# A fused pair-update and feed-forward kernel: the mix stage reads a transposed, normalized x stored by the projection stage instead of making its own

## What is computed

```
zn = LN(LN_c(x)); ppn, lpn, ipn = LN of the three other grids
ab1, ab2, ab3 = sigmoid(zn@Wg_k + bg_k) * (zn@W_k + b_k) * mask          (64 channels each)
pp, lp, ip    = the same form on the three others, without the mask
block = einsum('ikc,kjc->ijc', pp, ab1) + einsum('ikc,jkc->ijc', ab2, lp) + ab3*ip
g     = sigmoid(zn@Wend + bend)
x2    = x + g * (LN(block)@Wsum + bsum) * mask
t     = LN(x2); logits = mean(t)@Wr + br -> two of eight experts
out   = x2 + LN(t + expert mixture(t)) * gamma + beta
```

## Time and profile before

| | |
|---|---|
| time, median of 3 runs | 1593.93 us (1591.71 to 1597.03) |
| the profiled execution's own time | 1593.88 us |
| its span | 1592.1 us |
| PE busy | 1420.5 us (89%) |
| DVE busy | 1247.0 us (78%) |
| ACT busy | 1060.3 us (67%) |
| POOL busy | 1061.2 us (67%) |
| DMA | 232.66 MB, 347992 packets |

### The profile page before, as it was taken

One profiled execution on the slowest core, in us unless ns is written; L12 is line 12 of the kernel. 1 busy time (PEld: TensorE's weight loads), 2 busy tenths in 40 slices (PEclk: granted clock), 3 DMA queues, 4 the chain that ended last, 5 costly groups with the idle time before them and its releaser, 6 DMA issues. The chain is left out here.

```text
span 1592.1 us, 34869 instructions
## 1 busy us (share of the span) xinstructions
PE 1420.5 (89%) x10157; PEld 1186.6 (75%) x10157; DVE 1247.0 (78%) x4401; ACT 1060.3 (67%) x2439; POOL 1061.2 (67%) x1691
## 2 busy tenths in 40 slices
PE   6999999999999997787779999869999999999992
PEld 3877777777777776666657777649998888898882
DVE  7898888888888865555579999857788888888874
ACT  3877877877877883222279999734666667667662
POOL 4888888888888894333269999823555555555553
PEclk9999999999999998998989999969999999999996
DMA  9878789887899877676636665321222222222212
GB/s 197 201 180 200 183 205 225 203 192 179 188 206 222 207 201 215 191 244 174 175 86 176 167 179 166 107 74 37 67 80 67 79 79 69 76 79 66 80 41 79
DMA packets 347992, 232.66 MB, mean 146 GB/s; under 512 B 59558, under 2 KB 331902, under 8 KB 347838
## 3 DMA queue, kind: packets, MB, share of 16 engines
q1 hardware_dynamic: 346556, 230.40, 56.0%
q10 hardware_dynamic: 1010, 0.20, 0.1%
q0 software_dynamic: 272, 0.21, 0.1%
HBM read 155.28 MB, written 75.50 MB: 145 GB/s over the span
## 5 line engine op out<-in xcount | busy, mean ns | idle before, releaser
L616 PE MATMUL psZ_a<-w_all,xT_a 128*128 128x128 f32 (+1 forms) x2304 | 453.6, 336 | 33.9 <-ACT xT_a L526 23.3
L616 PEld LDWEIGHTS psZ_a<-w_all,xT_a 128*128 128x128 f32 x2304 | 316.1, 196 | 84.9 <-ACT xT_a L526 28.3
L1461 ACT ACTIVATE hT<-psH_d,b 128x512 f32<-128x512 f32 x288 | 197.7, 688 | 172.2 <-PE psH_d L1501 172.1
L1486 PE MATMUL psY_d<-w,hT 128*128 128x128 f32 x2304 | 268.9, 275 | 0.0
L1486 PEld LDWEIGHTS psY_d<-w,hT 128*128 128x128 f32 x2304 | 262.9, 192 | 0.1
L542 ACT ACTIVATE sig_a<-psZ_a 128x256 f32<-128x256 f32 (+1 forms) x360 | 153.4, 426 | 95.9 <-PE psZ_a L616 54.4
L1519 POOL TENSOR_TENSOR u_d<-u_d,gamma 128x512 f32<-128x512 f32 x72 | 95.6, 1328 | 159.9 <-ACT u_d L1447 142.3
L603 PE MATMUL psT_a<-ident,shared 128*128 128x128 f32 x1152 | 189.0, 277 | 4.2 <-issue 2.8
L603 PEld LDWEIGHTS psT_a<-ident,shared 128*128 128x128 f32 x1152 | 143.8, 144 | 55.5 <-issue 27.9
L554 POOL TENSOR_SCALAR shared<-shared,coefs_ix 128x128 f32<-128x128 f32 x348 | 154.0, 454 | 45.1 <-DVE coefs_ix L360 42.8
L526 ACT COPY xT_a<-psT_a 128x512 f32<-128x512 f32 (+1 forms) x360 | 175.9, 489 | 4.2 <-PE psT_a L603 2.5
(11 more groups left out here) (221 smaller groups left out, 3071.2 us busy)
## 6 DMA issues: line engine op xcount, KB each, us to landing
shared<-in_x_dram SPq DMA_DIRECT2D x48, 512.0 KB, 4.9
scratch_x<-x_c SPq DMA_DIRECT2D x36, 512.0 KB, 3.1
shared<-scratch_x SPq DMA_DIRECT2D x36, 512.0 KB, 3.6
shared<-in_x_dram SPq DMA_DIRECT2D x48, 256.0 KB, 4.3
shared<-L_conv_protein_pair_dram SPq DMA_DIRECT2D x24, 512.0 KB, 7.6
shared<-in_L_conv_l_pair_dram SPq DMA_DIRECT2D x24, 512.0 KB, 6.4
shared<-n_L_conv_inter_pair_dram SPq DMA_DIRECT2D x24, 512.0 KB, 6.4
scratch_ab<-low_ab SPq DMA_DIRECT2D x12, 1024.0 KB, 5.7
```

What stands on the lines that cost most here:

```text
L616: ins = nc.tensor.matmul(out, xT[:, G % 2, j * P:j * P + P], rhs[i], start=True, stop=True)
L1461: nc.scalar.activation(hT[:, g % 2, f, :], psH[:, f, :], ACT.Gelu, bias=s["b1"][:, f:f + 1]).then_inc(gelued, 1)
L1486: ins = nc.tensor.matmul(psY[:, g % 2, i * CH:i * CH + CH], hT[:, g % 2, f, i * P:i * P + P], s["w2"][:, f, :], start=(f == 0), stop=(f == ...
```

## The change

In the projection the copy of a turned x group goes to a buffer of a whole block, `xT_block`, from which PE multiplies and SP stores it to DRAM, a chunk at a time (8 tiles, 512 KB, rows of 4 KB per partition). In the mix stage `norm_x`, the two transposes of x and their part of the copy are gone, with DVE's copies of the coefficients; SP loads the turned tiles beside x itself, which is still added at the end. The wait of PE for the copy moves from ahead of the Wend product to ahead of the Wsum product. POOL, which no longer waits for x in `norm_x`, waits for it ahead of the sum.

```diff
 project_phase:
+        def turned_x(count, i, t0, size):
+            return xT_block[:, t0 * P:(t0 + size) * P] if i == 0 else xT[:, count % 2, 0:size * P]
...
+            def store_xT(n, k):
+                lo, hi = CHUNKS[k]
+                sp.wait_ge(copied, NG_A * n + hi // 2)
+                sp.dma_start(d["s_xT"][bass.ds(n, 1), :, lo * P:hi * P].rearrange("o p c -> (o p) c"),
+                             xT_block[:, lo * P:hi * P]).then_inc(stored_xT[k], 16)
...
                             load_third(i, k, n + 1)
+                            if i == 0:
+                                store_xT(n, k)
...
                         load_operands(OPERANDS[2 * i:2 * i + 2], 0, N - BLOCK_A)
+                        if i == 0:
+                            for k in range(len(CHUNKS)):
+                                store_xT(n, k)
...
+            for k in range(len(CHUNKS)):
+                sp.wait_ge(stored_xT[k], 16 * NBLK)
...
-                nc.scalar.copy(xT[:, count % 2, 0:size * P], psT[:, count % 2, 0:size * P]).then_inc(copied, 1)
+                if i == 0:
+                    for k, (lo, _) in enumerate(CHUNKS):
+                        if t0 == lo:
+                            need(act, stored_xT[k], 16 * (n + count // NG_A))
+                nc.scalar.copy(turned_x(count, i, t0, size), psT[:, count % 2, 0:size * P]).then_inc(copied, 1)
...
+def load_turned(eng, d, s, n, k):
+    lo, hi = CHUNKS[k]
+    eng.dma_start(mix_buffers(s)[1][:, n % 2, lo:hi, :].rearrange("p t c -> p (t c)"),
+                  d["s_xT"][bass.ds(n, 1), :, lo * P:hi * P].rearrange("o p c -> (o p) c")).then_inc(s["loaded_xT"][n % 2][k], 16)
...
 triangle_phase, SP:
                 for k, ch in enumerate(CHUNKS):
+                    load_turned(sp, d, s, p, k)
                     load_tiles(sp, mix_buffers(s)[0][:, p], d["x"], p, s["loaded_x"][p][k], ch)
...
 mix_phase, SP:
                     if j == hi // 2 - 1:
+                        if there(m + 1, par):
+                            sp.wait_ge(projected, PAIRS * n + hi // 2)
+                            load_turned(sp, d, s, n + 2, k)
                         sp.wait_ge(x2_made, PAIRS * n + hi // 2)
...
 ACT and POOL: every norm_x(...) is gone;
-                nc.scalar.copy(xT[:, j % 2, :], psT[:, j % 2, 0:3 * P]).then_inc(copied, 1)
+                nc.scalar.copy(triT[:, j % 2, :], psT[:, j % 2, 0:P]).then_inc(copied, 1)
...
                 if 2 * j == CHUNKS[k][0]:
                     need(pool, stored[par][k], 16 * m)
+                    pool.wait_ge(loaded_x[par][k], 16 * CHUNK_DMAS[k] * (m + 1))
...
 PE:
-                for i in range(2):
-                    nc.tensor.transpose(psT[:, j % 2, i * P:i * P + P], xh[:, j % 4, i, :], s["ident"][:])
...
-                    pe.wait_ge(copied, c + 1)
+                    k = CHUNK_OF[2 * j]
+                    if 2 * j == CHUNKS[k][0]:
+                        pe.wait_ge(s["loaded_xT"][par][k], 16 * (m + 1))
                     need(pe, gated, c - 1)
                     for i in range(2):
-                        ins = nc.tensor.matmul(psZ[:, j % 2, CH * i:CH * i + CH], xT[:, j % 2, i * P:i * P + P], w_end,
+                        ins = nc.tensor.matmul(psZ[:, j % 2, CH * i:CH * i + CH], xT_in[:, par, 2 * j + i, :], w_end,
                                                start=True, stop=True)
                     ins.then_inc(projected, 1)
+                    pe.wait_ge(copied, c + 1)
                     need(pe, y_made, c - 1)
...
 DVE: coef_x_of(...), L1096, is gone
```

More of the change, by code:

```diff
@@ L426, in project_phase @@
         stored = [sem("stored_ab"), sem("stored_pp"), sem("stored_lp")]
+        stored_xT = [sem(f"stored_xT_{k}") for k in range(len(CHUNKS))]
         setup = setup_parts(nc, d, s, ctx, psZ[:].rearrange("p a b c -> p (a b) c"))
@@ L615, in body @@
                         out = psZ[:, G % 3, j, 0:6 * HID] if i == 0 else psZ[:, G % 3, 0, j * P:j * P + P]
-                        ins = nc.tensor.matmul(out, xT[:, G % 2, j * P:j * P + P], rhs[i], start=True, stop=True)
+                        ins = nc.tensor.matmul(out, turned_x(G, i, t0, size)[:, j * P:j * P + P], rhs[i], start=True, stop=True)
                     ins.then_inc(projected, 1)
@@ L713, in mix_buffers @@
     shared = s["shared"]
-    X, H = 2 * TPB * CH, 8 * CH
-    return (shared[:, 0:X].rearrange("p (r t c) -> p r t c", r=2, t=TPB),
-            shared[:, X:X + H].rearrange("p (r t c) -> p r t c", r=4, t=2))
+    X = 2 * TPB * CH
+    return tuple(shared[:, X * k:X * k + X].rearrange("p (r t c) -> p r t c", r=2, t=TPB) for k in range(2))
+def load_turned(eng, d, s, n, k):
+    lo, hi = CHUNKS[k]
+    eng.dma_start(mix_buffers(s)[1][:, n % 2, lo:hi, :].rearrange("p t c -> p (t c)"),
+                  d["s_xT"][bass.ds(n, 1), :, lo * P:hi * P].rearrange("o p c -> (o p) c")).then_inc(s["loaded_xT"][n % 2][k], 16)
 def ffn_inputs(s):
@@ L951, in _ @@
                     sp.wait_ge(stored[par][k], 16 * NBLK // 2)
[L953 to L964, removed]
         def norm_tri(wait, op, sem_out, m, par, j, which):
@@ L990, in slot @@
                 if three:
-                    norm_x(act.wait_ge, op, normed_act, *three, 0)
                     norm_tri(act.wait_ge, op, tri_normed_act, *three, 0)
@@ L1017, in slot @@
                 if three:
-                    norm_x(wait, op, normed_pool, *three, 1)
                     norm_tri(wait, op, tri_normed_pool, *three, 1)
@@ L1029, in _ @@
             for j in range(3):
-                norm_x(wait, op, normed_pool, 0, 0, j, 1)
                 norm_tri(wait, op, tri_normed_pool, 0, 0, j, 1)
@@ L1057, in slot @@
                         turn(*one)
-                    pe.wait_ge(copied, c + 1)
+                    k = CHUNK_OF[2 * j]
+                    if 2 * j == CHUNKS[k][0]:
+                        pe.wait_ge(s["loaded_xT"][par][k], 16 * (m + 1))
                     need(pe, gated, c - 1)
                     for i in range(2):
-                        ins = nc.tensor.matmul(psZ[:, j % 2, CH * i:CH * i + CH], xT[:, j % 2, i * P:i * P + P], w_end,
+                        ins = nc.tensor.matmul(psZ[:, j % 2, CH * i:CH * i + CH], xT_in[:, par, 2 * j + i, :], w_end,
                                                start=True, stop=True)
                     ins.then_inc(projected, 1)
+                    pe.wait_ge(copied, c + 1)
                     need(pe, y_made, c - 1)
-                    nc.tensor.matmul(psW[:, j % 2, 0:2 * CH], xT[:, j % 2, 2 * P:3 * P], s["ws2"][:], start=True, stop=True
+                    nc.tensor.matmul(psW[:, j % 2, 0:2 * CH], triT[:, j % 2, :], s["ws2"][:], start=True, stop=True
                                      ).then_inc(tri_projected, 1)
@@ L1146, in slot @@
                     if part == 1 and now:
-                        if j == 0 and ahead:
-                            coef_x_of(*next_block(m, par))
                         c = PAIRS * n + j
@@ L1162, in slot @@
                             stats_tri(*pair)
-            coef_x_of(0, 0)
             for j in range(PAIRS):
@@ L1655, in metaformer_kernel @@
     d["s_lp"] = scratch("scratch_lp", (N, NCG, N * CC))
+    d["s_xT"] = scratch("scratch_xT", (NBLK, P, TPB * P))
     d["s_x2"] = scratch("scratch_x2", (NBLK, P, TPB * CH))
@@ L1669, in metaformer_kernel @@
         s["loaded_x"] = [chunk_sems(f"loaded_xc{par}") for par in range(2)]
+        s["loaded_xT"] = [chunk_sems(f"loaded_xT{par}") for par in range(2)]
         s["operands_loaded"] = [ctx.enter_context(nc.semaphore(f"loaded_{k}")) for k in ("even", "odd")]
```

16 lines of the change are left out of this document (4 added, 12 removed).

## The result

The kernel after takes 1568.32 us (median of 4 runs, 1565.22 to 1569.84), the kernel before 1595.48 us in the same series (1591.71 to 1598.94). The ratio is 0.9825, with an interval of 0.9811 to 0.984: 27 us or 1.75% faster. 1576 was predicted, with a range of 1565 to 1589. The profiled executions are 24.0 us apart in their spans, 1592.1 and 1568.1.

A forecast was written before the change was run, and what follows sets the result against it. The prediction took POOL in the mix stage to bound the kernel. Mix blocks -23.1, start -0.8, projection blocks +2.2 and last block +3.7 gave -18.0 us, so 1576 us, range 1565 to 1589.

The forecast's parts named there:

- POOL is the bound of the kernel before: Mix stage: POOL needs 1.58 us a slot with almost no idle time, so it sets the pace; DVE follows.
- Step slots at 1.45, 10.4 together: Mix stage, seven slots with chain steps: 1.45 us each, with 0.25 for the first slot 10.4 for 11.05 a block.
- The ring: Mix stage: y, handover, POOL's sum, rest of the DVE step held by that sum, next step, y: 1.45 us.
- Light slots at POOL's 1.12, 5.6: Mix stage, five slots without chain steps: POOL's 1.12 us each, so 5.6 for 6.66 a block.
- The sum of 16.2: Mix block: 16.0 us from its slots plus 0.2 for handovers that do not mesh, against 18.31.
- Mix stage as a whole: Mix blocks 1 to 11 gain 2.1 us each, 23.1 together; block 0 keeps its time.
- Start: Start of the mix stage: norms of x leave the queue ahead of the first tri copy, 0.8 us gained.
- xT arrives in time: Mix stage: loads issued over a block (16 us) early, DMA 14.5 of 16.2 us, so PE should not wait.
- Projection blocks +2.2: Projection: the added stores cost 0.2 us in each of 11 blocks, 2.2 us; bounds 0 and 14.
- Rival 2: Projection: store backlog survives the x pass, lp arrives late, DVE stands; 3.7 us a block, 1615 us; chance 0.08.
- Last block +3.7: Projection's last block: three stores behind the operand loads lie on the path, 3.7 us; bounds 0 and 5.
- rival 3: Mix stage: the hold of DVE's steps by POOL's sum goes too; blocks 15.2 us, total 1565 us; chance 0.07.

The follow-up runs named there:

- kernel with stores alone: The kernel before plus the buffer xT_block and the projection's stores of it, which nothing reads: 1599.84 us against 1595.66, ratio 1.0024.
- kernel with loads alone: The kernel after without the projection's stores; the mix stage loads as many bytes of x itself in place of xT: 1563.6 us, 0.9793 of the kernel before.
- the spread steps: The kernel after with the last block's stores issued early and the coefficient chain over eight slots instead of seven: 1562.86 us, 0.9796 of the kernel before.
- short-sum kernel: The kernel after with POOL's sum reading y alone, the residual x left out: 1562.22 us (one run).

## Why the prediction held, point by point

- **POOL is the bound of the kernel before.** Shown: its norm put back costs the whole gain (18.52). But POOL alone was worth less than half of it: without its norm PE is the bound, 1.1 us a block lower (17.37).
- **Step slots at 1.45, 10.4 together.** Right in size (1.45, 10.28). The ring is shown by the missing tri bn_stats (no gain, hold longer) and by block 10. The prediction missed that DVE's own queue is as long, and so took the ring as the only bound: wherever the tri bn_stats run, a shorter sum does not shorten the slot (1.50 for 1.45).
- **Light slots at POOL's 1.12, 5.6.** Right in size (5.69), and partly by luck. POOL's slots are shorter (910.03 - 905.73 = 4.30 us for four sums, 1.075 each), and what ends the five slots is PE: from the first of them on it has no idle time, and in slot 0 of each block y waits 0.40 us for it. The prediction had put PE's 0.11 a slot at nothing, since the buffers let it be ahead; the lead does not last to the end. The two errors nearly cancel. The sum of 16.2 was 0.2 too high: 0.1 in the step slots, and of the 0.2 for handovers 0.1 was needed.
- **Mix stage as a whole.** The rest of the stage gave 28.0 for 23.1. Ten blocks gave 2.4 each instead of 2.1; block 11 gave 16.09 - 14.05 = 2.0; block 0 gave 23.16 - 21.64 = 1.5 where nothing was predicted.
- **Start.** -1.2 for -0.8, inside the bounds given (0 to 1.4).
- **xT arrives in time.** The mix stage's DMA share is 0.95 (0.90 worked out), and no wait of PE on a load is in the list of its waits.
- **Projection blocks +2.2.** Not seen. PE's projection ends at 595.01 in one profile of the kernel after and at 596.40 in the other, for 596.56 before, and over all twelve profiles between 594.9 and 600.2, so the profiles can't settle 2 us; the time of the kernel with stores alone leaves little room for it. Rival 2 is out. The x pass had room, its share rose from 0.00 and 0.55 to 0.25 and 0.79. DVE's wait on the load of lp (answers to the earlier trace rows) grew from 2.0 to 5.0 us, just at the bound that was set. It is no sign of the stores: it is 3.6 in the second profile, and 6.9 in the kernel with loads alone, which has none.
- **Last block +3.7.** The wait for the first load of the triangle grew from 8.1 to 12.1 us, 4.0 (12.0 in the second profile). In the first profile PE's projection happens to end 1.5 us early, so the triangle starts only 2.4 later; in the second it starts 3.7 later.
- **Not foreseen: the triangle is 3.1 us longer** (1.4 in the second profile of the same kernel). The kernel with loads alone has it as well, that with stores alone does not (189.2). Over all profiles it is 186.8 to 189.2 us with the mix stage of before (four profiles), 189.7 to 192.3 with that of after (eight). The loads of x and xT, 3 MB more, run beside the last group: the window 792 to 798 us has DMA share 1.08, that of before 0.00. They explain only a part. The first of them is issued at 779.85, 4.7 us into the last group, and by the start of that group 168.1 us of the stage had passed for 165.6 before: 2.5 of the 3.1 us come ahead of the loads. Behind them lies the last handover to the mix stage's first matmul, 0.8 longer (1.95 for 1.17). In all eight profiles the mix stage starts 0.69 us after SyncE has issued the last of these loads (798.23 here), 1.2 to 2.6 us after PE's last matmul of the triangle; with the mix stage of before SyncE is done some 7 us earlier and the handover is 1.17 in all four. What adds the time ahead of the last group stays open (165.3 to 167.0 us against 166.4 to 168.4 over all profiles).

So the blind sum of -18 was made of -23.9 and +5.9; the spans show -29.2 in the mix stage, +5.5 in front of it, and -0.3 behind. With 1568.32 us the time is nearer to rival 3's 1565 than to the forecast 1576, but not by rival 3's mechanism: blocks are at 15.97 us and not 15.2, and the held step is there in block 10.

## What to carry to other kernels

When an operation is taken from all engines at once, the new time of a slot is that of the longest loop left over, and it can be read from before's timeline: y, its handover, the other engine's instruction, the held step. Compute every engine's own queue as well as the loop, over a whole block too: an engine that is slower by a tenth of a us a slot uses up the lead that its buffers give. Where two agree to a hundredth, shortening one gives nothing, and work has to move to slots with room, as the spread steps do. A transfer that is issued early gives back a part of its gain if its own wait holds back the transfers behind it in the same queue. Compare a start time with a profile of the same series: that of the triangle moved by 1.3 us between two profiles of one kernel.

## What the runs showed of the hardware

The prediction said that POOL's norms do not hold DVE's steps. That was too quick. The following counts are over the mix stages of all twelve profiles, for the chain's steps on 128x48 (all but L145 and L152). Of the steps that start under POOL's sum of y and x, 0.24 to 0.36 us behind its start, all 133 are held: they last 0.43 to 0.55 us instead of the 0.16 to 0.21 of a step with no POOL instruction beside it, and end 0.03 to 0.07 us after the sum.

Of the steps that start under a norm of POOL, the 574 that come 0.06 to 0.13 us behind its start last 0.15 to 0.22 and end ahead of it, so they are not held. Of the 162 that come 0.14 to 0.22 us behind it, 151 last 0.24 to 0.34 and end 0.03 to 0.06 after it. The other 11, all in the short-sum kernel, are not held; there the norm lasts 0.45 to 0.47 us instead of 0.40. The early steps cost POOL something too: in the kernel after a tri norm with such a step lasts 0.43 us, one with no step beside it 0.40 (medians). The step of the short-sum kernel above is one of the 151: it starts at 900.13, the norm beside it ends at 900.31, the step at 900.37.

```profile
899.92 0.39 POOL L1024 TENSOR_SCALAR tri_n<-tri,coefs_c 128x64 f32<-128x64 f32 x1
```

So POOL's norms hold DVE's steps as its sum does, and under a norm the moment at which the step comes decides: up to 0.13 us behind the norm's start it passes. The same line, L161, is in both groups: 0.21 us long when it comes 0.12 behind the norm, 0.29 at 0.18. Whether a step can pass under the sum as well is open. Only two come as early there, both L145 (96 columns, 0.09 behind), and both are held (0.82 and 0.83 us). The Trainium skill, page "SBUF — State Buffer", section "Who interferes with whom", says that whoever issues first has the shared ports for the whole instruction. By these rows that holds for steps that come 0.24 us and more behind POOL's sum, and for 151 of the 162 that come 0.14 to 0.22 us behind a norm; a step that comes almost together with a norm goes first.
